# Pad rows written two tiles earlier and wider, and step counts read later, in a routed audio tower

## The chip, the cores and the metric

The kernel runs on one core of one Trainium2 chip. The metric is device time in microseconds, the median of several executions. TensorE (PE) multiplies, VectorE (DVE) and ScalarE (ACT) do elementwise work, GpSimd (POOL) does small scalar work and indirect transfers, SyncE (SP) issues ordinary transfers. Every engine follows its own list of instructions and meets the others at semaphores.

## The reference, cut to what matters

64 sequences of 125 tokens with 192 features pass through a token block (depthwise convolution, pointwise product, pooling to 62 tokens, a Fourier transform, a norm), attention with relative positions, a quantised feed-forward, a second local attention, and a mixture of experts. The change is at the border before the last part. There every token chooses one of 8 experts, whose gated feed-forward is applied to it alone:

```python
route = jax.nn.softmax(hidden_states @ router_w + router_b, axis=2)
max_prob = jnp.max(route, axis=2).reshape(-1, 1)
max_ind = jnp.argmax(route, axis=2).reshape(-1)
for e in range(N_EXPERTS):
    xe = jnp.where(mask, x, 0.0)
    oe = jax.nn.silu(xe @ w1[e]) * (xe @ w2[e]) @ w3[e]
out = out.astype(jnp.bfloat16) * max_prob
```

## The kernel before, in words

**First phase.** `TILES` is 32: a tile is two sequences, 124 real tokens in 128 lanes. `overlapped` runs the stages of all parts as a software pipeline, and each engine has its stages in an order written out by hand. Tiles are numbered 0 to 31. Three short stages at the end of the pipeline route a tile's tokens: `r_route` makes the logits, `r_choose` the one-hot choice, and `r_slots` on VectorE gives every token a row in the DRAM tensor `routed`, where each expert owns a region of `CAP` rows. `filled` holds the next free row of each region. `r_scatter` on GpSimd then writes the tile's rows to `routed` with an indirect transfer, from `moe_row`. That buffer is single, so `r_normalise_in` of the next tile waits on ScalarE for the scatter's landing (`r_scattered`). After the last router product TensorE runs `fill_bank(38)`, 38 products of the identity that nobody reads, and earlier fills of the same kind (`last_turns`) stand ahead of some stages of the last two tiles.

**Pad rows.** The experts work on whole blocks of 128 rows, so the rows behind each region's last token must hold pad rows. VectorE copies `filled` to `pads_at` in `r_slots` of tile 30, SyncE reads the eight places and writes two blocks (256 rows of 1,544 bytes) at each, and the scatter of tile 31 waits for all eight (`pads_written`), since it overwrites some of the pad rows with real ones.

**Plan and second phase.** After `r_slots` of tile 31 VectorE computes `plan`: for each expert step its expert and its first row, and the number of steps, here 34. `planned` releases all engines into `staggered`. Each engine reads three registers from `plan` (number of steps, last step, last but one: a `value_load` each), runs three peeled steps, then a loop over the rest, then the two closing steps. A step has three lagged parts: x (load 128 rows to `e_tok`, transpose, copy to `e_xT`, copy the expert's weights), g (two products to a hidden width of 512, and the gate: `e_gate_up`, `e_tanh_gate`, `e_silu`) and y (`e_down`, `e_finish`, `e_scatter`). In the peeled steps PE's list is: transpose of step 0; gate and up of step 0, transpose of step 1; gate and up of step 1, transpose of step 2, down of step 0. Then the loop opens with gate and up of step 2. SyncE waits for all 32 scatters before `staggered`, so before it reads any register.

Of the kernel before, what the change touches and what calls it, by code (L numbers as in the profile page):

```python
# [17 lines left out]
P = 128  # L18
TILES = NB // 2
# [17 lines left out]
NC = D // 2 + 1  # L37
CAP = 4224
MAX_TILES = TILES + NE
EARLY = 4  # L40
MAGIC = 1.5 * 2.0 ** 23
EPS = 1e-5
# [2 lines left out]
ROW = 2 * D + 2  # L45
# [4 lines left out]
def first(m):  # L50

    return isinstance(m, int) and m == 0
# [8 lines left out]
class Chain:  # L61
# [6 lines left out]
    def stage(self, name, m):  # L68
        if first(m):
            self.starts[name] = self.n  # L70
            return
        if self.per_tile is None:
            self.per_tile = self.n
        self.base, self.n = m * self.per_tile + self.starts[name], 0
# [14 lines left out]
def audio_tower(nc, x, taps, w_pw, b_pw, dft, dft_seq, gamma, beta,  # L89
# [3 lines left out]
    routed = nc.dram_tensor("routed", ((NE + 1) * CAP, ROW), FP32).ap()  # L93
# [3 lines left out]
    with ctx:  # L97
        def sb(name, shape, dt=FP32, mem=None):
            return (mem or ctx).enter_context(nc.sbuf_tensor(name, shape, dt))

        def sem(name):
            return ctx.enter_context(nc.semaphore(name))
# [5 lines left out]
        c_region = sb("c_region", [P, NE + 1])  # L108
        c_steps = sb("c_steps", [P, MAX_TILES])
        pad_rows = sb("pad_rows", [P, ROW])  # L110
        w3_sb = sb("w3_sb", [P, NE, HID1 // P, D])
        EXPERT, FIRST_ROW, STEPS = 0, MAX_TILES, 2 * MAX_TILES
        plan = sb("plan", [P, STEPS + 3], I32)
# [5 lines left out]
        earlier_tiles = sb("earlier_tiles", [P, NE + 1, NE])  # L119
        reached = sb("reached", [P, NE - 1, MAX_TILES])  # L120
        jumped = sb("jumped", [P, NE - 1, MAX_TILES])
        pads_at = sb("pads_at", [P, NE], I32)
# [6 lines left out]
        def lp(name, shape, dt=FP32):  # L129
            return sb(name, shape, dt, loop_mem)  # L130

        lp("early_weights", [P, EARLY, 3, HID1])

# [119 lines left out]
        def bank(name):  # L253
# [57 lines left out]
        planned, pads_written, pads_placed, w_early = (sem(k) for k in ("planned", "pads_written", "pads_placed", "early_weights_landed"))  # L311
        (e_loaded, e_xpose, e_xTr, e_lo_set, e_hi_set, e_g, e_u, e_tanhr, e_gated, e_yr, e_o, e_rested, e_final, e_turn, e_stored, all_stored) = (sem(f"e_{k}") for k in (
            "x_loaded", "transposed", "xT_ready", "low_weights_set", "high_weights_set", "gate_done", "up_done", "tanh_ready",
            "gated", "y_ready", "down_done", "rest_loaded", "row_final", "row_turn", "stored", "all_stored"))
        GE = NE - EARLY
        w_late = {e: sem(f"weights_landed_from_{e}") for e in range(EARLY, NE, GE)}
        w_ready = sem("expert_weights_ready")
        w_spare = sb("w_spare", [P, NE])

        def staggered(eng, stages):  # L320


            lag = {"x": 0, "g": 1, "y": 2}
            eng.wait_ge(planned, 1)
            total, last, last_but_one = (
                eng.value_load(plan[0:1, STEPS + k:STEPS + k + 1], min_val=TILES - 1 - k, max_val=MAX_TILES - k) for k in range(3))  # L326

            def body(steps):
                for name, stage in stages:
                    if name in steps:  # L330
                        stage(steps[name])
            for j in range(E_PEELED):
                body({name: j - late for name, late in lag.items() if j >= late})
            with eng.Fori(E_PEELED, total) as j:  # L334
                body({name: j - late for name, late in lag.items()})
            body({"g": last, "y": last_but_one})
            body({"y": last})
            return total
# [8 lines left out]
        def load_weights(queue, es, landed):  # L347

            for part, src, r in ((0, w1, slice(0, KB)), (1, w2, slice(KB, P))):
                queue.dma_start(w_sb[:, es, part, :], src[es, 0:P, :].rearrange("e p n -> p e n")).then_inc(landed, 16)  # L350
                queue.dma_start(w_sb[r, es, 2, :], src[es, P:D, :].rearrange("e p n -> p e n")).then_inc(landed, 16)
# [22 lines left out]
        def _(sp):  # L374
# [69 lines left out]
            sp.wait_ge(pads_placed, 1)  # L444
            for e in range(NE):
                at = sp.value_load(pads_at[0:1, e:e + 1], min_val=0, max_val=NE * CAP)  # L446
                sp.dma_start(routed[bass.ds(at, 2 * P), :].rearrange("(a p) w -> p a w", p=P),  # L447
                             pad_rows[:, :].unsqueeze(1).broadcast_to([P, 2, ROW])).then_inc(pads_written, 16)
            sp.wait_ge(r_scattered, 16 * TILES)

            def first_row(j):
                at = plan[0:1, FIRST_ROW + j:FIRST_ROW + j + 1] if isinstance(j, int) else plan[0:1, bass.ds(j + FIRST_ROW, 1)]
                return sp.value_load(at, min_val=0, max_val=NE * CAP)

            def load_rows(j):
                src = routed[bass.ds(first_row(j), P), 0:D]
                if not first(j):
                    sp.wait_ge(e_xpose, j)
                sp.dma_start(e_tok[:, :], src).then_inc(e_loaded, 16)

# [10 lines left out]
        def _(pool):  # L471
# [5 lines left out]
            for t_ in (kBD, p0, f_xqT, vBD, qT1, kBD_hi, p1, oT1, b_xT, r_xT):  # L477
                a = t_[tuple(slice(None) for _ in t_.shape)]
                last = pool.memset(a, 0.0)
# [31 lines left out]
            def spare_of(k):  # L511
                at = ("scatter", "rows").index(k)
                return pool_spare[:, at:at + 1]
# [41 lines left out]
            def r_scatter(m):  # L555
                pool.wait_ge(r_slot, m + 1)
                pool.wait_ge(r_row, m + 1)
                pool.wait_ge(b_kept, m + 1)
                if isinstance(m, int) and m == TILES - 1:
                    pool.wait_ge(pads_written, 16 * NE)  # L560

                pool.tensor_tensor(out=spare_of("scatter"), in0=half[:, :], in1=half[:, :], op=ALU.add)
                pool.indirect_dma_start(out=routed, out_offset=bass.IndirectOffsetOnAxis(ap=slot_now[:, 0:1], axis=0),  # L563
                                        in_=moe_row[:, :], in_offset=None).then_inc(r_scattered, 16)
# [4 lines left out]
            def mark_weights(landed, es):  # L569
                pool.wait_ge(landed, 64)  # L570
                for e in es:
                    pool.tensor_tensor(out=w_spare[:, e:e + 1], in0=half[:, :], in1=half[:, :], op=ALU.add).then_inc(w_ready, 1)  # L572
            mark_weights(w_early, range(EARLY))
            pool.wait_ge(r_scattered, 16 * TILES)
# [16 lines left out]
        def _(pe):  # L591
            def mm(dst, lhsT, rhs, start=True, stop=True):
                return nc.tensor.matmul(dst, lhsT, rhs, start=start, stop=stop)  # L593
# [29 lines left out]
            def fill_bank(times):  # L623

                pe.wait_ge(t_yread, TILES)
                for k in range(times):
                    mm(pt[:, 0:P], ident[:, :], ident[:, :])
# [262 lines left out]
            def r_rank(m):  # L890
# [9 lines left out]
                (2, a_add_relative), (1, t_dft_seq), (4, b_probs_transpose), (5, r_rank), (2, a_probs_transpose),  # L900
                (4, b_values), (2, a_values), (3, f_transpose_y), (4, b_transpose_o), (3, f_down),
                (2, a_transpose_heads), (4, b_output), (1, a_transpose)))
            fill_bank(38)

            def e_transpose(j):
                pe.wait_ge(e_loaded, 16 * j + 16)
# [33 lines left out]
        def _(act):  # L940
# [48 lines left out]
            def t_copy_z(m):  # L989
                if isinstance(m, int) and m == 2:  # L990
                    act.dma_start(w3_sb[:, :, :, :], w3.rearrange("e (k p) d -> p e k d", p=P)).then_inc(w_e, 16)
                    load_weights(act, slice(0, EARLY), w_early)
                act.wait_ge(t_z, 2 * m + 2)
# [196 lines left out]
        def _(dve):  # L1190
# [258 lines left out]
            def r_slots(m):  # L1449

                c = ch["r"]
                c.stage("slots", m)
                dve.wait_ge(r_ranked, m + 1)
                c.link(v.tensor_tensor(place[:, :], filled[:, :], pa0[:, RK:RK + NE + 1], ALU.add))
                c.link(v.tensor_tensor(filled[:, :], filled[:, :], pa0[:, TT:TT + NE + 1], ALU.add))
                v.scalar_tensor_tensor(place_one[:, :], place[:, :], 1.0, chosen[:, :], ALU.mult, ALU.mult,
                                       accum_out=slot_f[:, :]).then_inc(r_read, 1)
                dve.wait_ge(r_read, m + 1)
                dve.wait_ge(r_sum, m + 1)
                if isinstance(m, int) and m == TILES - 2:  # L1460
                    v.tensor_copy(pads_at[:, :], filled[:, 0:NE]).then_inc(pads_placed, 1)
                after_previous(dve, r_scattered, 16 * m)
                v.tensor_copy(slot_now[:, :], slot_f[:, :]).then_inc(r_slot, 1)
                at = c_tokens[:, m:m + 1] if isinstance(m, int) else c_tokens[:, bass.ds(m, 1)]
                v.tensor_copy(moe_row[:, TOKEN:ROW].bitcast(I32), at)
                v.reciprocal(moe_row[:, PROB:PROB + 1], exp_sum[:, :]).then_inc(r_row, 1)
# [23 lines left out]
            def by_step(t):  # L1490
                return t[:, 1:NE].unsqueeze(2).broadcast_to([P, NE - 1, MAX_TILES])
            plan_step(v.tensor_tensor(reached[:, :, :], c_steps[:, :].unsqueeze(1).broadcast_to([P, NE - 1, MAX_TILES]),
# [149 lines left out]
```

## Time and profile before

| | |
|---|---|
| median of 3 runs | 1183.44 us (1182.4 to 1183.57) |
| the profiled execution's own time | 1182.29 us |
| its span in the profile | 1180.4 us |
| PE busy | 1025.5 us (87%) |
| ACT busy | 835.4 us (71%) |
| DVE busy | 791.3 us (67%) |
| POOL busy | 363.6 us (31%) |
| mean granted TensorE clock | 0.98 |

Times in the rows are microseconds from the start of the span. A share of busy time is a mean over stages: the first phase takes about 985 us, the second some 190, and between them lies the stretch that the change touches, where the engines wait for one another.

### The profile page before, as it was taken

Reading aid. Unit: us, or ns where it says so; the run is one execution under the profiler, and the core shown is the slowest. Engines: PE = TensorE matmul, PEld = TensorE weight load, DVE = VectorE, ACT = ScalarE, POOL = GpSimd, SP = SyncE. Lnnn points to the kernel's source line nnn. Section 1 sums busy time; section 2 is a strip of 40 time slices with the busy share of each in tenths; the row PEclk is TensorE's granted clock in tenths of the full one; section 3 lists DMA queues with packets and bytes.
Section 4 is the critical chain, followed back from the end, with each engine's and each line's share of the span. In section 5 each row is a group of like instructions: output and inputs, shape, how many; then the busy total and the mean of one; then the engine's idle time right before and its main releaser. Section 6 shows DMA issues by size and latency. Waiting matters only on the chain. (4 is left out here: it accounts for less than half of the span.)

```text
span 1180.4 us, 31803 instructions
## 1 busy us (share of the span) xinstructions
PE 1025.5 (87%) x9700; PEld 787.8 (67%) x9733; DVE 791.3 (67%) x2641; ACT 835.4 (71%) x2673; POOL 363.6 (31%) x1096
## 2 busy tenths in 40 slices
PE   3748989999899999999888999989998887999995
PEld 2636666666666666666666666666666677888885
DVE  2346777777777777777777777777775542555553
ACT  2437888888888888888888888888887541333332
POOL 2012233333333333333333333333333211122222
PEclk9878999999999999999999999999999898999999
DMA  6153111111111111111111111111111403122221
GB/s 221 34 174 106 34 41 39 42 42 39 39 39 39 56 40 47 44 39 39 39 39 39 39 46 39 39 39 39 47 48 39 118 8 128 50 59 58 57 60 42
DMA packets 74258, 65.67 MB, mean 56 GB/s; under 512 B 39341, under 2 KB 63696, under 8 KB 74096
## 3 DMA queue, kind: packets, MB, share of 16 engines
q1 hardware_dynamic: 64832, 49.58, 14.3%
q0 software_dynamic: 3680, 9.38, 2.2%
q10 hardware_dynamic: 5712, 6.29, 1.8%
q8 instruction: 18, 0.29, 0.1%
q14 instruction: 16, 0.13, 0.0%
HBM read 36.57 MB, written 28.95 MB: 56 GB/s over the span
## 5 line engine op out<-in xcount | busy, mean ns | idle before, releaser
L1239 DVE SCALAR_TENSOR_TENSOR conv_lo<-xT_lo,c_taps,conv_lo 128x248 f32<-128x248 f32 x192 | 89.7, 467 | 14.9 <-ACT xT_hi L942 14.9
L1184 ACT ACTIVATE e_tanh<-bank_a 128x512 f32<-128x512 f32 x34 | 20.3, 597 | 104.7 <-PE bank_a L593 104.7
L1134 ACT ACTIVATE p<-bank_b,max 128x62 f32<-128x62 f32 x384 | 81.1, 351 | 0.2 <-DVE max L1404 0.2
L501 POOL TENSOR_TENSOR var_y<-ssq_y,c_eps 128x1 f32<-128x1 f32 x32 | 6.0, 189 | 233.6 <-ACT f_sq L1104 233.6
L593 PE MATMUL bank_a<-e_xT,w_now 128*128 128x128 f32 x544 | 70.5, 284 | 5.8 <-DVE e_gate L1516 1.5
L593 PEld LDWEIGHTS bank_a<-e_xT,w_now 128*128 128x128 f32 x544 | 64.9, 196 | 14.9 <-issue 12.0
L593 PE MATMUL bank_a<-c_wv,a_xT 64*64 64x384 f32 (+1 forms) x512 | 74.0, 503 | 0.0
L593 PE MATMUL bank_a<-a_xT,c_wq 64*128 64x128 f32 (+1 forms) x512 | 71.7, 282 | 0.0
L593 PE MATMUL bank_a<-c_wo,oT 128*128 128x192 f32 x384 | 68.5, 329 | 0.3 <-ACT oT L942 0.2
L593 PE MATMUL bank_a<-a_xT,c_wk 64*128 64x128 f32 (+1 forms) x512 | 68.8, 280 | 0.0
L593 PEld LDWEIGHTS bank_a<-a_xT,c_wq 64*128 64x128 f32 (+1 forms) x512 | 64.3, 191 | 4.3 <-ACT a_xT L942 0.4
L1404 DVE TENSOR_REDUCE max<-bank_b 128x8 f32<-128x496 f32 x64 | 31.9, 540 | 50.2 <-PE bank_b L593 50.2
L1243 DVE SCALAR_TENSOR_TENSOR conv_hi<-xT_hi,c_taps,conv_hi 128x124 f32<-128x124 f32 x192 | 65.4, 340 | 0.0
L593 PEld LDWEIGHTS bank_a<-c_wo,oT 128*128 128x128 f32 x384 | 62.1, 191 | 1.3 <-ACT oT L942 0.8
L1511 DVE COPY w_now<-w_sb 128x512 f32 x34 | 14.5, 427 | 71.9 <-PE bank_a L593 68.8
L593 PEld LDWEIGHTS bank_a<-a_xT,c_wk 64*128 64x128 f32 (+1 forms) x512 | 62.1, 190 | 0.0
L1040 ACT ACTIVATE p<-bank_a,max 128x62 f32<-128x62 f32 x256 | 55.5, 331 | 7.7 <-DVE max L1301 7.7
L593 PEld LDWEIGHTS bank_t<-z_sb,c_dft_seq 128*128 128x128 f32 x256 | 32.7, 199 | 34.4 <-ACT z_sb L942 33.9
L593 PE MATMUL bank_b<-c_wqkv,b_xT 128*128 128x288 f32 x128 | 39.6, 432 | 16.1 <-ACT b_xT L942 16.0
L593 PE MATMUL bank_b<-w_sb,e_y 128*128 x272 | 50.0, 327 | 2.1 <-DVE e_row L1531 2.0
L593 PEld LDWEIGHTS bank_a<-c_wv,a_xT 64*64 64x64 f32 (+1 forms) x512 | 22.3, 133 | 36.5 <-issue 36.5
L593 PE MATMUL bank_t<-z_sb,c_dft_seq 128*128 128x95 f32 (+1 forms) x256 | 37.9, 293 | 9.3 <-ACT z_sb L942 8.3
(264 smaller groups left out, 3059.5 us busy)
## 6 DMA issues: line engine op xcount, KB each, us to landing
rel_scores<-rel_tok SPq DMA_DIRECT2D x32, 492.0 KB, 2.6
rel_skew<-rel_scores SPq DMA_DIRECT2D x64, 124.0 KB, 3.0
x_tok<-in_x SPq DMA_DIRECT2D x32, 187.5 KB
e_rest<-routed SPq DMA_DIRECT2D x34, 97.0 KB, 1.9
e_tok<-routed SPq DMA_DIRECT2D x34, 96.0 KB, 2.0
routed<-pad_rows SPq DMA_DIRECT2D x8, 386.0 KB, 3.8
w_sb<-in_w ACTq DMA_DIRECT2D x1, 3072.0 KB, 12.3
w_sb<-in_w ACTq DMA_DIRECT2D x2, 1024.0 KB, 13.7
```

The lines of the kernel that those rows point to most:

```text
L501: pool.tensor_tensor(out=var[k][:, :], in0=ssq[k][:, :], in1=c_eps[:, width:width + 1], op=ALU.mult).then_inc(var_eps[k], 1)
L593: return nc.tensor.matmul(dst, lhsT, rhs, start=start, stop=stop)
L1040: last = nc.scalar.activation(p0[:, h, 0:T], pa1[:, h * T:(h + 1) * T], ACT.Exp, bias=max0[:, h:h + 1])
L1134: last = nc.scalar.activation(p1[:, h, 0:T], src[:, at * T:(at + 1) * T], ACT.Exp, bias=max1[:, mx:mx + 1])
L1184: nc.scalar.activation(e_tanh[:, :], pa0[:, :], ACT.Tanh, scale=0.5).then_inc(e_tanhr, 1)
L1239: c.mark(v.scalar_tensor_tensor(conv_lo[:, :, :], xT_lo[:, :, k:k + PAIRS], c_taps[:, 0, k:k + 1], conv_lo[:, :, :], ALU.mult, ALU.add))
L1243: ins = v.scalar_tensor_tensor(conv_hi[:, :], xT_hi[:, k:k + PAIRS], c_taps[:, 1, k:k + 1], conv_hi[:, :], ALU.mult, ALU.add)
L1404: last = v.tensor_reduce(max1[:, lo:lo + n], src[:, 0:n * T].rearrange("p (h s) -> p h s", h=n), axis=AX.X, op=ALU.max, negate=True)
L1511: v.tensor_copy(w1_now[:, :], weights_of(e, 0)).then_inc(e_lo_set, 1)
```

## The change

Three edits. First, the pad rows' places are taken in `r_slots` of tile 29 and not of tile 30; since two more tiles can now fill rows behind them, three blocks are written at each place and not two; and the scatter of tile 30 waits for them, not that of tile 31. Second, `staggered` reads its three registers behind the three peeled steps on every engine, and SyncE's wait for the 32 scatters moves into `load_rows` of step 0, behind the reading of its first row. Third, the last fill is 33 products and not 38.

```diff
+PADDED_AT, PAD_BLOCKS = TILES - 3, 3
...
             eng.wait_ge(planned, 1)
-            total, last, last_but_one = (
-                eng.value_load(plan[0:1, STEPS + k:STEPS + k + 1], min_val=TILES - 1 - k, max_val=MAX_TILES - k) for k in range(3))
...
             for j in range(E_PEELED):
                 body({name: j - late for name, late in lag.items() if j >= late})
+            total, last, last_but_one = (
+                eng.value_load(plan[0:1, STEPS + k:STEPS + k + 1], min_val=TILES - 1 - k, max_val=MAX_TILES - k) for k in range(3))
             with eng.Fori(E_PEELED, total) as j:
...
-                sp.dma_start(routed[bass.ds(at, 2 * P), :].rearrange("(a p) w -> p a w", p=P),
-                             pad_rows[:, :].unsqueeze(1).broadcast_to([P, 2, ROW])).then_inc(pads_written, 16)
-            sp.wait_ge(r_scattered, 16 * TILES)
-
+                sp.dma_start(routed[bass.ds(at, PAD_BLOCKS * P), :].rearrange("(a p) w -> p a w", p=P),
+                             pad_rows[:, :].unsqueeze(1).broadcast_to([P, PAD_BLOCKS, ROW])).then_inc(pads_written, 16)
...
-                if not first(j):
+                if first(j):
+                    sp.wait_ge(r_scattered, 16 * TILES)
+                else:
                     sp.wait_ge(e_xpose, j)
...
-                if isinstance(m, int) and m == TILES - 1:
+                if isinstance(m, int) and m == PADDED_AT + 1:
                     pool.wait_ge(pads_written, 16 * NE)
...
-            fill_bank(38)
+            fill_bank(33)
...
-                if isinstance(m, int) and m == TILES - 2:
+                if isinstance(m, int) and m == PADDED_AT:
                     v.tensor_copy(pads_at[:, :], filled[:, 0:NE]).then_inc(pads_placed, 1)
```

## Rows read from the trace of the kernel before

**Rows 1.** Timeline of ACT, `r_normalise_in` of tiles 30 and 31.
```profile
961.79 0.55 ACT L1066 ACTIVATE moe_row<-res_m,norm_shift_b,rstd_b 128x192 f32<-128x192 f32 x1
...
980.25 0.55 ACT L1066 ACTIVATE moe_row<-res_m,norm_shift_b,rstd_b 128x192 f32<-128x192 f32 x1 [5.74 <-DMA routed<-moe_row,slot_now]
```
**Rows 2.** Timeline of POOL; in brackets the idle time before and its releaser.
```profile
975.24 1.04 POOL L563 DMA_INDIRECT routed<-moe_row,slot_now  x1 [0.49 <-issue]
...
977.62 0.19 POOL L525 TENSOR_TENSOR norm_shift_b<-neg_mean_b,rstd_b 128x1 f32<-128x1 f32 x1
989.18 0.19 POOL L562 TENSOR_TENSOR pool_spare<-half 128x1 f32<-128x1 f32 x1 [11.37 <-DMA routed<-pad_rows]
...
992.66 1.01 POOL L572 TENSOR_TENSOR w_spare<-half 128x1 f32<-128x1 f32 x4 [1.10 <-DMA routed<-moe_row,slot_now]
```
**Rows 3.** Timeline of SP, merged: first start and time to the last.
```profile
975.72 9.79 SPq L447 DMA_DIRECT2D routed<-pad_rows  x8
994.97 9.96 SPq L459 DMA_DIRECT2D e_tok<-routed  x3
```
**Rows 4.** Chain of waits, 980 to 1016: start, us, what ran.
```profile
985.13 3.89 DMA routed<-pad_rows
```
**Rows 5.** Timeline of DVE: start, us, engine, line, operation, out<-in.
```profile
952.74 0.15 DVE L1463 CAST slot_now<-slot_f 128x1 int32<-128x1 f32 x1 [0.97 <-DVE place_one L1456]
...
974.06 0.17 DVE L1461 CAST pads_at<-filled 128x8 int32<-128x8 f32 x1
...
984.85 0.15 DVE L1466 RECIPROCAL moe_row<-exp_sum 128x1 f32<-128x1 f32 x1
...
989.30 0.20 DVE L1503 CAST plan<-plan_f 128x83 int32<-128x83 f32 x1
```
**Rows 6.** Timeline of PE around the border of the two phases.
```profile
975.32 3.96 PE L593 MATMUL bank_t<-ident 128*128 128x128 f32 x34
980.85 0.44 PE L596 MATMUL bank_a<-ident,moe_row 128*128 128x128 f32 x2 [1.58 <-ACT moe_row L1066]
...
983.93 8.73 PE L593 MATMUL bank_t<-ident 128*128 128x128 f32 x76
996.96 0.44 PE L596 MATMUL bank_t<-ident,e_tok 128*128 128x128 f32 x2 [4.30 <-DMA e_tok<-routed]
...
1005.93 2.02 PE L593 MATMUL bank_a<-e_xT,w_now 128*128 128x128 f32 x16 [1.51 <-DVE e_gate L1516]
```
**Rows 7.** Stretches: us, then busy us of PE, PEld, DVE, ACT, POOL; PEclk, DMA share, GB/s.
```profile
976.00:988.00 12.00, 10.12 (x88) 9.55 (x87) 5.10 (x26) 1.63 (x6) 1.35 (x5) 1.00 0.79 282
915.40:922.20 6.80, 4.14 (x35) 2.80 (x34) 4.69 (x12) 6.40 (x27) 0.93 (x3) 1.00 1.02 274
905.10:911.90 6.80, 4.70 (x38) 2.69 (x34) 3.87 (x12) 6.20 (x20) 2.55 (x11) 1.00 0.18 74
922.20:929.00 6.80, 6.53 (x75) 5.75 (x76) 2.69 (x14) 3.58 (x9) 0.98 (x2) 0.50 0.69 191
...
998.20:1004.02 5.82, 5.82 (x33) 5.37 (x34) 0.00 (x0) 0.60 (x1) 0.00 (x0) 0.50 0.06 17
1010.82:1013.97 3.15, 3.15 (x33) 2.91 (x34) 1.44 (x4) 0.10 (x2) 1.01 (x2) 1.00 0.18 46
```
**Rows 8.** Instructions reading `plan`: ns min/median/max, first and last start (us).
```profile
L453 SPq TENSOR_LOAD <-plan x68: 262/268/281, 994.3 to 1164.9; - x68
```
**Rows 9.** Line L326, the three register reads of each engine, same columns.
```profile
L326 DVEq SEQ_ASSERT  x3: 23/23/41, 990.4 to 991.6; - x3
L326 PEldq TENSOR_LOAD <-plan x3: 305/492/545, 990.6 to 992.4; - x3
...
L326 PEldq SEQ_ASSERT  x3: 18/18/28, 991.4 to 993.0; - x3
```
**Rows 10.** Line L334, setting up and running the loop, 1005 to 1016.
```profile
L334 PEldq MOVE  x3: 34/38/43, 1009.2 to 1014.8; - x3
```
**Rows 11.** Line L342, the reading of a step's expert, 985 to 1016.
```profile
L342 DVEq SEQ_ASSERT  x4: 23/23/23, 992.3 to 1012.6; - x4
```

## The prediction

> **What bounds the kernel now.** I read the chain of waits first, then the timelines of each engine from 950 to 1016, then the instructions that read `plan`, then busy time by stretch. The first phase (to about 985) and the expert loop (from gate and up of step 2, then a steady 1010.82 − 1005.93 = 4.9 us per step [rows 6, 7]) have TensorE almost always busy, and no edit touches what a step does. What the edits can win lies in the border between them. There the reader sees four waits in a row.
>
> First, `r_normalise_in` of tile 31 starts at 980.25, after 5.74 us of idle ScalarE, and what releases it is the landing of tile 30's scatter [rows 1]. That scatter was issued at 975.24, half a microsecond before the first pad write [rows 2, 3], and shared the transfer engines with them. Its own operand was ready at 977.62 + 0.19 = 977.81 [rows 2].
> Second, the last pad write is issued at 985.13 and lands 3.89 later [rows 4]; only then, at 989.18 after 11.37 idle, does GpSimd begin tile 31's scatter [rows 2], though its row was complete at 984.85 + 0.15 = 985.00 [rows 5]. It lands before 992.66 [rows 2], so 3.48 after its start, with little else in flight.
> Third, SyncE wakes there, reads three registers and a first row, and issues the first `e_tok` at 994.97 [rows 3]. The plan had stood since 989.30 + 0.20 = 989.50 [rows 5].
> Fourth, TensorE has run out of fills, waits 4.30 us, starts the first transpose at 996.96 [rows 6], and does gate and up of step 0 at a granted clock of 0.50 in 5.82 us, where step 2 has 1.00 and 3.15 us [rows 7].
>
> **Edit 1, pads by tile 29's places.** The copy to `pads_at` moves from 974.06 to about 952.74 [rows 5]. The first pad write followed it by 975.72 − 974.06 = 1.66 [rows 3], so it now goes out at 954.4. Eight writes of 3 × 128 × 1,544 bytes are 4.74 MB against 3.16 MB. In 976 to 988 the engines moved 282 GB/s at a busy share of 0.79 [rows 7]; at that rate 4.74 MB take 16.8 us, and with about 1.5 us ahead of the first packets the last lands near 972.7. Tile 30's scatter starts its first instruction at 974.5. So the new wait costs nothing, by 1.8 us. Bounds: at the mean of the old series, 3.16 MB in 989.02 − 975.72 = 13.3 us, it is 20 us and lands at 974.4, still in time; at a full share of 282/0.79 = 357 GB/s it lands near 969. Queued behind that wait on GpSimd is `b_scale` of tile 31, for which `r_normalise_in` waits, but TensorE is in fills until 975.32 + 3.96 = 979.28 [rows 6], which covers the first half microsecond or so of lateness.
> The writes now collide with tile 29's scatter. Tile 30's, so disturbed, landed 980.25 − 975.24 = 5.0 after issue. Tile 29's goes out near 953.9; at 5.0 it lands at 958.9, and even at 5.0 × 1.5 at 961.4, while `r_normalise_in` of tile 30 starts at 961.79 for other reasons [rows 1]. Cost nothing, cover 0.4 to 2.9 us.
> Tile 30's scatter now lands 3.48 after its first instruction at 974.55, at 978.03, so `moe_row` starts 2.2 earlier. Not all of it arrives: the transposes that started 0.60 after it, at 980.85 [rows 6], would start at 978.63 but stand behind the fills to 979.28. Gain 980.85 − 979.28 = **1.57**, carried through logits, ranks, `r_slots` and the plan, which is ready at 987.93. The scatter of tile 31 starts 0.14 behind its row, at 983.57, and lands at 987.05, before the plan.
>
> **Edit 2, registers behind the peeled steps.** SyncE now goes from the plan to the first row. Reading it and issuing takes 994.97 − 994.3 = 0.67 [rows 3, 8]. A first read after the same wake-up can be slow: 545 ns on TensorE against 305 [rows 9], so up to 0.24 more. I take 0.77: `e_tok` goes out at 988.70, and its scatter wait is met since 987.05. That is 6.27 earlier than 994.97, so beyond the 1.57 it is **4.70**. VectorE's first weights, which had the three reads ahead of them too, come earlier by as much as is needed, and ScalarE's are far ahead.
> The reads themselves come back later. TensorE's took from 990.6 to 993.0, 2.4 us, in three of 305 to 545 ns and their arithmetic [rows 9]. Its sequencer has given out all of step 0's down product by 1009.2 [rows 10], 1.6 us before the array starts gate and up of step 2 at 1010.82 [rows 7]. If the reads take 1.9 us (three at 305 ns) to 2.4, that start slips by 0.4 to 1.0, with 0.1 to 0.2 to dispatch. VectorE's reads end at 991.6 [rows 9], 2.1 after the plan; behind its step-2 work they push the expert's reading, done at 1012.6 before [rows 11], to 1014.4 to 1014.7, 0.2 to 0.5 past its need at about 1014.2 (TensorE ends step 2's products at 1013.97 [rows 7]), and lie beside TensorE's delay. SyncE's, ScalarE's and GpSimd's lie in idle time. I take **−0.6**; bounds are 0, all hidden, and −2.4, TensorE's reads in full.
> The Trainium skill, "TensorE: Matmul & The Clock Gate", section "Architectural detail: the array is 16× 32×32, not 1× 128×128", gives TensorE a queue of 64 entries, so its sequencer could run far ahead and the reads would cost nothing; the sum would then be 0.6 larger, 1174.5. The trace agrees that it runs ahead, but by the 1.6 us above.
>
> **Edit 3, fills.** 38 took 8.73, so 0.230 each [rows 6]; 33 take 7.58 and end at 983.93 − 1.57 + 7.58 = 989.94. The first transpose, with `e_tok` landing as before 1.99 after issue, starts at 990.69. TensorE idles 0.75 and not 4.30, then 0.8 for ScalarE's copy as before. The granted clock was 1.00 until the long idle, so I expect gate and up of step 0 at 1.00: 5.82 − 3.15 = **2.67**. Bounds: 0 and 2.67.
>
> **Sum.** 1.57 + 4.70 + 2.67 − 0.6 = 8.34. The profiled execution took 1182.29, 1.89 more than its span of 1180.4; it would take 1173.95. It is 1.15 below the median of the runs, 1183.44, so the median becomes 1183.44 − 8.34 = **1175.1**, 0.7% less. This kernel's measurement tells about 0.2%, 2.4 us, from no change.
>
> **Rivals.**
> *The clock falls later* (0.28). The low clock of 922.2 to 929 followed no long idle, only a stretch with 4.14 us of matmuls in 6.8; after 4.70 in 6.8 it stayed at 1.00 [rows 7]. From the end of the fills to gate and up of step 1 (1005.93 before [rows 6], now 996.99) there would be 0.44 + 3.15 + 0.5 = 4.1 in 7.05. That resembles the stretch before a fall. Step 1 would then run low in place of step 0, giving 2.67 back and a little of the down product: 2.9, so 1178.0. For it speaks that stretch; against it that the fills before are dense. It may differ between executions. The Trainium skill, same page, section "HAM oscillation — how this bites in real kernels", blames long waits of TensorE between its bursts; none of the new gaps (0.75, 0.8, 1.5) is as long as 4.30, so by that rule the clock stays and 1175.1 holds.
> *Reads in series* (0.06). TensorE's 2.4 and VectorE's 2.1 add instead of overlapping: −4.5 in place of −0.6, 1179.0. Against it: VectorE had its expert's number 1.6 us ahead of its need [rows 11], and that slack takes most of its reads.
> *Pads late* (0.07). If the bigger writes run at 200 GB/s they land near 978.1 with their start, 2.9 past what costs nothing: 1178.0.
> *Slower than before* (0.02). The same wait, worse: all of 8.34 is gone when pads land near 983.5, 29 us after their first issue, an average of 163 GB/s. Rows show 238 over the old series, so it decides only below two thirds of that.
> *The gain does not come* (0.04). Something else releases the first `e_tok`, for instance SyncE held by full queues, and only what the scatter gains remains: around 1181.
>
> **Chances and range.** Forecast 0.53; its own range is 1174.0 to 1176.8, from reads at 0 to −1.0, a first read between 0.67 and 0.91 and half a microsecond of spread between medians. With the clock rival, the series and the late pads, 1173.6 to 1179.3 leaves out about 1 in 10. Faster by over 0.2% (below 1181.1) 0.94, within 0.04, slower 0.02.
>
> **What would show it.** Right: pads issued from about 954.4 and landed before 974.5; `moe_row` of tile 31 at about 978.0, the transposes at 979.3; plan at 987.9; first `e_tok` at 988.7, first transpose at 990.7 with under 1 us idle; gate and up of step 0 in 3.2 us at 1.00; a gap of 0.4 to 1.0 on TensorE ahead of gate and up of step 2, and 4.9 per step after. Wrong: GpSimd idle on pads ahead of tile 30's scatter, `moe_row` of tile 30 released by a transfer, a granted clock of 0.50 after 990, or a step period other than 4.9.

## The result and the profile after

Six executions of the changed kernel have a median of 1175.02 us (1174.04 to 1176.97), six of the kernel before 1183.11 (1182.4 to 1183.57). The ratio is 0.9934, 95% interval 0.9921 to 0.9947. The profiled execution took 1174.49 us with a span of 1172.7. The forecast was 1175.1.

In this execution the whole border sits later by 962.28 − 961.79 = 0.49. `moe_row` of tile 29 was already 0.47 later (938.20 against 937.73), and the first instruction that an edit moves, the copy to `pads_at`, ran at 953.24, so this offset is not the edits' doing. So below I measure from `moe_row` of tile 30, the first of these two rows (the timeline of ScalarE, beside [rows 1]):

```profile
962.28 0.55 ACT L1067 ACTIVATE moe_row<-res_m,norm_shift_b,rstd_b 128x192 f32<-128x192 f32 x1
...
978.76 0.55 ACT L1067 ACTIVATE moe_row<-res_m,norm_shift_b,rstd_b 128x192 f32<-128x192 f32 x1 [3.75 <-DMA routed<-moe_row,slot_now]
```

Tile 30's is released by no transfer, so the collision of the larger writes with tile 29's scatter cost nothing. Tile 31's is still released by the scatter of tile 30, but 16.48 us behind tile 30's row and not 18.46. That scatter now lands 978.76 − 975.99 = 2.77 after it was issued, where it took 5.01 with the pad writes behind it [rows 1, 2]. The timeline of GpSimd (beside [rows 2]):

```profile
974.99 0.20 POOL L563 TENSOR_TENSOR pool_spare<-half 128x1 f32<-128x1 f32 x1 [15.28 <-DVE moe_row L1467]
975.99 1.04 POOL L564 DMA_INDIRECT routed<-moe_row,slot_now  x1 [0.81 <-issue]
...
978.13 0.19 POOL L526 TENSOR_TENSOR norm_shift_b<-neg_mean_b,rstd_b 128x1 f32<-128x1 f32 x1
983.85 0.20 POOL L563 TENSOR_TENSOR pool_spare<-half 128x1 f32<-128x1 f32 x1 [5.53 <-DVE moe_row L1467]
...
987.31 0.63 POOL L573 TENSOR_TENSOR w_spare<-half 128x1 f32<-128x1 f32 x4 [0.82 <-DMA routed<-moe_row,slot_now]
```

Both scatters now start when VectorE has made their row (the brackets name `moe_row`), neither waits for pads, and the second lands before 987.31, ahead of the plan. VectorE and SyncE (beside [rows 5] and [rows 3]):

```profile
988.08 0.20 DVE L1504 CAST plan<-plan_f 128x83 int32<-128x83 f32 x1
```
```profile
954.90 11.86 SPq L448 DMA_DIRECT2D routed<-pad_rows  x8
989.02 7.32 SPq L460 DMA_DIRECT2D e_tok<-routed  x3
```

The first `e_tok` follows the plan by 989.02 − 988.28 = 0.74, where 5.47 lay between them [rows 3, 5]. The pad writes land 4.2 to 5.6 after issue, so the last, issued at 966.4, by 972.0, 3 us before the scatter of tile 30 could want them:

```profile
L448 SPq DMA_DIRECT2D routed<-pad_rows x8: 372/372/415, 954.9 to 966.4; - x8
...
DMA to landing us min/median/max: 4.2/5.3/5.6
```

TensorE (beside [rows 6]):

```profile
975.82 3.96 PE L594 MATMUL bank_t<-ident 128*128 128x128 f32 x34
979.61 0.38 PE L597 MATMUL bank_a<-ident,moe_row 128*128 128x128 f32 x2
...
982.64 7.61 PE L594 MATMUL bank_t<-ident 128*128 128x128 f32 x66
991.05 0.41 PE L597 MATMUL bank_t<-ident,e_tok 128*128 128x128 f32 x2 [0.80 <-DMA e_tok<-routed]
992.32 2.05 PE L594 MATMUL bank_a<-e_xT,w_now 128*128 128x128 f32 x16 [0.86 <-ACT e_xT L943]
...
997.25 2.02 PE L594 MATMUL bank_a<-e_xT,w_now 128*128 128x128 f32 x16 [1.41 <-DVE e_gate L1517]
...
1003.14 2.02 PE L594 MATMUL bank_a<-e_xT,w_now 128*128 128x128 f32 x16 [1.11 <-DVE e_gate L1517]
```

The router's transposes stand directly behind the fills. The wait for `e_tok` is 0.80 and not 4.30. Gate and up of step 0 run at full clock (stretches, beside [rows 7]):

```profile
992.32:995.50 3.18, 3.18 (x33) 2.94 (x34) 0.00 (x0) 0.64 (x2) 0.00 (x0) 1.00 0.12 31
```

What is new is the gap of 1.11 ahead of gate and up of step 2. It is TensorE's register reads (beside [rows 9] and [rows 10]):

```profile
L334 PEldq TENSOR_LOAD <-plan x3: 302/311/317, 1000.8 to 1002.1; - x3
...
L334 PEldq SEQ_ASSERT  x3: 18/18/18, 1001.4 to 1002.7; - x3
...
L334 DVEq TENSOR_LOAD <-plan x3: 298/304/310, 1003.4 to 1004.6; - x3
```
```profile
1001.68 0.68 DVE L1517 SCALAR_TENSOR_TENSOR e_gate<-e_tanh,bank_a 128x512 f32<-128x512 f32 x1
...
1003.11 1.86 PEld L594 LDWEIGHTS bank_a<-e_xT,w_now 128*128 128x128 f32 x16 [1.38 <-issue]
```

The gap's bracket in the timeline of TensorE names `e_gate` of step 1, but that was ready at 1002.36. In the kernel before the next product follows `e_gate` by 0.14, here by 0.78, and the weight load ahead of it waited for nothing but its own issue. VectorE's reads begin at 1003.4, when gate and up already run.

From gate and up of step 3 to the end of the span it is 1172.7 − 1008.05 = 164.65 us, against 1180.4 − 1015.72 = 164.68. The loop is the same.

### The profile page after: what moved, and what is told of

It is laid out like the page before. It is cut to its first block and busy times, and to the rows that moved or that the text cites. A ratio compares the mean times of both kernels' runs of the same rounds, so it can differ in the third digit from the quotient of the medians.

```text
span 1172.7 us, 31784 instructions
## 1 busy us (share of the span) xinstructions
PE 1022.0 (87%) x9690; PEld 784.3 (67%) x9723; DVE 791.9 (68%) x2641; ACT 836.8 (71%) x2673; POOL 364.9 (31%) x1096
```

## The experiments

All from the changed kernel unless said. The times come from three chips: one for the first four kernels below (pads only, reads only, SyncE behind, 38 fills), one for 14 fills, the gap fills, 15 fills and five blocks, one for the tiny fills, 24 fills, the changed kernel again and the last one. On them the kernel before has medians of 1186.1 to 1187.6 and spreads over 4.8 to 6.9 us, not 1183.1 and 1.2 as in the first result, so I give ratios to the kernel before on the same chip, and beside them a length from each profile: the **border**, from `moe_row` of tile 30 to the start of gate and up of step 3. It is 1015.72 − 961.79 = 53.93 in the kernel before and 1008.05 − 962.28 = 45.77 in the changed one. One profile is one execution, so what the clock did in it is told too. A **fall** is a stretch in which the granted clock drops from 1.00 to 0.50.

### Edit 1 alone, edit 2 alone

Pads only is the kernel before, with

```diff
+PADDED_AT, PAD_BLOCKS = TILES - 3, 3
...
-                if isinstance(m, int) and m == TILES - 1:
+                if isinstance(m, int) and m == PADDED_AT + 1:
...
-                if isinstance(m, int) and m == TILES - 2:
+                if isinstance(m, int) and m == PADDED_AT:
```

and `PAD_BLOCKS` blocks in place of two in each pad write. Reads only is the kernel before, with the two lines of `total, last, last_but_one` moved behind the peeled steps, and

```diff
-            sp.wait_ge(r_scattered, 16 * TILES)
...
-                if not first(j):
+                if first(j):
+                    sp.wait_ge(r_scattered, 16 * TILES)
+                else:
```

Both keep the 38 fills of the kernel before.

> Edit 1 alone: places taken in tile 29, three blocks, scatter of tile 30 waits; the registers are read ahead of the peeled steps and there are 38 fills, as before. My theory: the pads' wait held both the scatter of tile 31 and, by collision, moe_row of tile 31, so the plan comes 1.3 to 1.6 us earlier and SyncE, now released by the plan, reads three registers (1.65) and a first row (0.7): first e_tok some 4.5 us earlier than in the kernel before, fills end after the landing of the plan and leave about 1 us idle, the clock stays at 1.00 (2.67): together about 7 us, ratio 0.994. Rival, that the late reading on SyncE was the main bound: then this alone gives 2 us or less, ratio 0.998.

> Edit 2 alone: registers behind the peeled steps and SyncE's wait for the scatters behind the first row's reading; pads as before, 38 fills. My theory: the scatter of tile 31 still lands at about 992.6, the first e_tok goes out 0.3 behind it, 2.0 us earlier than before; TensorE pays 1.0 us ahead of gate and up of step 2; the idle behind the fills shrinks from 4.3 to 2.3 us, so the clock may or may not fall: gain 1 us with the fall, 3.7 without, ratio 0.999 or 0.997. Rival: with the reads out of the way the gain is as large as that of both edits, ratio 0.993.

Measured: pads only 0.9938 (0.9917 to 0.9959), reads only 0.9980 (0.9967 to 0.9993). The timelines of SyncE, first of pads only and then of reads only:

```profile
992.24 8.90 SPq L460 DMA_DIRECT2D e_tok<-routed  x3
```
```profile
993.66 7.31 SPq L459 DMA_DIRECT2D e_tok<-routed  x3
```

From `moe_row` of tile 30 (963.82 and 962.87) the first `e_tok` goes out after 28.42 and 30.79, against 33.18 before and 26.74 with both: 4.8 earlier by the pads alone, 2.4 by the reads alone, 6.4 by both. The pads were the main bound, as the first expectation says. The collision is told apart too: tile 30's scatter landed 2.78 after issue with the pads moved (977.51 to 980.29) and 4.76 with the pads as before (976.33 to 981.09). The borders are 49.77 and 49.90. The profile of pads only had the clock fall twice, in steps 0 and 1, which cost 1.8 and 1.6 (6.71 and 6.49 between starts of gate and up, where the undisturbed ones are 4.93 and 4.90). That of reads only had it fall once, at 982 to 988, among the fills. There it cost little, since the slow fills took time in which TensorE would have waited: the wait for `e_tok` was 0.97, not the 2.3 expected, and gate and up of step 0 ran at 1.00. So the two borders don't compare the edits, the `e_tok` times do. The ratios set reads only apart from both edits, but not pads only (0.9938 against 0.9934): what edit 2 adds to edit 1 is seen in the traces and not in the times. In reads only the gap ahead of step 2 was there too: 5.99 between gate and up of steps 1 and 2.

### Which reads may stand behind

Four engines read the counts ahead of the peeled steps again, and SyncE alone behind them:

```diff
-        def staggered(eng, stages):
+        def staggered(eng, stages, ahead=True):
+            def step_counts():
+                return [eng.value_load(...) for k in range(3)]
+            if ahead:
+                total, last, last_but_one = step_counts()
...
-            total, last, last_but_one = (
+            if not ahead:
+                total, last, last_but_one = step_counts()
...
-            staggered(sp, (("x", load_rows), ("y", load_rest)))
+            staggered(sp, (("x", load_rows), ("y", load_rest)), ahead=False)
```

> The changed kernel, but only SyncE reads its registers behind the peeled steps; the other four read them ahead, TensorE in the time of its fills. My theory: the 1.0 us gap ahead of gate and up of step 2 goes, and nothing takes its place, since VectorE (reads 2.1, expert 0.9, weights 0.85 after the plan) has the first weights just as e_xT is ready: 1 us under the changed kernel, about 1174.0, ratio to the kernel before 0.9925. Rival: VectorE's first weights come late by up to 1 us and the time stays at that of the changed kernel.

Measured: 0.9926 (0.9910 to 0.9943). Its profile has 4.90 between gate and up of steps 1 and 2, so the gap is gone. VectorE (its timeline) has the first weights ready at 991.95 + 0.42 = 992.37, and gate and up start at 992.59:

```profile
991.60 0.43 DVE L1516 COPY w_now<-w_sb 128x512 f32 x1 [3.02 <-issue]
991.95 0.42 DVE L1517 COPY w_now<-w_sb 128x512 f32 x1
```

So the rival's late VectorE didn't come, by 0.2 us. But in this execution the clock fell in gate and up of step 0 (6.66 between starts, 1.7 lost), and the border is 46.46. The gain of 1.0 is clear in the trace; the ratios of 0.9926 and 0.9934 don't tell it from nothing. The edit took the reads away from four engines at once; that TensorE's were the ones that counted is read from the timeline of the changed kernel above.

### The fills and the clock

The changed kernel with another number of fills ahead of step 0, here 38, below 14 and 24:

```diff
-            fill_bank(33)
+            fill_bank(38)
```

> The changed kernel with 38 fills in place of 33. The five fills take 1.15 us and end 0.35 us behind the landing of e_tok: 0.3 us slower than the changed kernel if fills only fill, with no idle behind them. If the busy time of TensorE in the border decides the clock in some executions (the changed kernel's runs spread over 2.9 us), the spread narrows and the median is the same or up to 0.5 us lower.

Measured: 0.9930 (0.9909 to 0.9950), border 45.98, 0.2 longer than with 33; no fall in the border. So edit 3 is worth nearly nothing by itself. In four executions the spread was 2.1.

> The changed kernel with 14 fills behind the router and not 33, so that TensorE idles about 5 us ahead of the first transpose. Nothing else waits for the fills. My theory (2.67 of the gain was the clock): the granted clock is 0.50 during gate and up of step 0, which takes 5.8 us in place of 3.2, and the kernel is 2.7 us slower than the changed one: ratio to the kernel before 0.9957. From the moe_row of tile 30 to gate and up of step 3 the changed kernel takes 45.8 us; this takes 48.4. Rival, the shorter idle bought nothing by itself: no difference, ratio 0.993.

Measured: 1.0063 (1.0041 to 1.0085), 15 us slower than the changed kernel, where 2.7 was expected. The border accounts for little of it: 47.76, 2.0 longer, from 5.10 of idle and a low clock in the first half of step 0. The rest is in the loop: 30 steps from gate and up of step 3 take 163.91 and not 146.87 (149.2 to 150.9 in the other kernels on this chip). Nearly every one takes about 5.47 and not 4.90. Lines of its timeline for one such step:

```profile
1024.91 0.17 PEld L597 LDWEIGHTS bank_t<-ident,e_tok 128*128 128x128 f32 x2
...
1025.02 0.60 ACT L1185 ACTIVATE e_tanh<-bank_a 128x512 f32<-128x512 f32 x1 [2.71 <-PE bank_a L594]
...
1025.72 0.43 DVE L1512 COPY w_now<-w_sb 128x512 f32 x1 [2.36 <-PE bank_a L594]
...
1026.40 0.68 DVE L1517 SCALAR_TENSOR_TENSOR e_gate<-e_tanh,bank_a 128x512 f32<-128x512 f32 x1
...
1027.23 2.18 PE L594 MATMUL bank_a<-e_xT,w_now 128*128 128x128 f32 x16 [0.57 <-DVE e_gate L1517]
```

And of the same place in a step of the changed kernel:

```profile
1020.98 0.60 ACT L1185 ACTIVATE e_tanh<-bank_a 128x512 f32<-128x512 f32 x1 [3.02 <-PE bank_a L594]
...
1021.23 0.43 DVE L1512 COPY w_now<-w_sb 128x512 f32 x1 [1.77 <-PE bank_a L594]
...
1021.91 0.68 DVE L1517 SCALAR_TENSOR_TENSOR e_gate<-e_tanh,bank_a 128x512 f32<-128x512 f32 x1
```

ScalarE answers TensorE's gate and up at once in both. VectorE starts the next weights 0.25 behind ScalarE's tanh in the changed kernel and 0.70 with 14 fills. `e_gate` stands behind the weights on VectorE, and TensorE waits for it. The change that was made touches TensorE's code ahead of the loop only.

> The changed kernel with 4 full fills and 29 products of one column by one column behind the router: as many instructions on TensorE as with 33 fills, but only some 3 us of work, so that it idles 4 us or more ahead of the first transpose. With 14 fills the steps of the loop took 5.45 us in place of 4.90, because VectorE woke 0.45 later after TensorE's gate and up. Theory A, the number of instructions on TensorE ahead of the loop decides that (where its code lies): here steps take 4.90 again and only the clock's price is left, about 2.7 us, ratio 0.9957. Theory B, the idle time or the fall of the clock ahead of the loop sets the rhythm of the steps: 5.45 again, ratio about 1.006.

```diff
-            fill_bank(33)
+            fill_bank(4)
+            for k in range(29):
+                mm(pt[0:1, 0:1], ident[:, 0:1], ident[:, 0:1])
```

Measured: 0.9947 (0.9928 to 0.9966), border 47.95. Five of its 30 steps take about 5.44 and the others 4.90. TensorE idled longer than with 14 fills, and the low clock lasted longer:

```profile
981.67 2.66 PE L594 MATMUL bank_t<-ident 128*128 128x128 f32 x66
990.17 0.66 PE L597 MATMUL bank_t<-ident,e_tok 128*128 128x128 f32 x2 [5.85 <-DMA e_tok<-routed]
991.70 3.79 PE L594 MATMUL bank_a<-e_xT,w_now 128*128 128x128 f32 x16 [0.86 <-ACT e_xT L945]
995.41 1.18 PE L594 MATMUL bank_a<-e_xT,w_hi_now 64*128 64x128 f32 x16
```

So theory B falls, as far as one profile and four executions on another chip can tell: neither the idle time nor the clock sets the rhythm of the steps. What is left is the number of TensorE's instructions ahead of the loop, or something that follows from it. The price of the idle time is here 2.2 of border (47.95 against 45.77), below the 2.7 expected, since the clock came back before the second half of step 0's products. It is a price only against an execution without a fall; the second profile of the changed kernel, below, has 47.57.

> The changed kernel with 24 fills. TensorE idles about 2.9 us ahead of the first transpose. Theory A (number of instructions): steps between 4.90 and 5.45, depending on where the code comes to lie; theory B (idle time): a fall of the clock in about half of the executions and with it 5.45. Without either: ratio 0.9945, the clock's price in half of the executions.

Measured: 0.9959 (0.9946 to 0.9973), border 47.56, with the clock low in gate and up of step 0 (6.52 between starts) after 2.86 idle. Eight of 30 steps are slow, where the other kernels on these chips have four to seven. So if the number of instructions acts, it does not act evenly: with 14 fills nearly every step is slow, with 24, 33 and 38 few are.

The changed kernel was then run once more on one of these chips, with no edit.

> The changed kernel itself, on the chip of the other three: ratio to the kernel before 0.9934 as at first. Its own profile tells how often a step takes 5.45 here, and whether the clock falls in the border.

Measured: 0.9932 (0.9916 to 0.9949), as at first. But its profile is not the first one. The border is 47.57, 1.8 longer, in the same code, after an idle of 0.94 where the first had 0.80. The stretch of gate and up of step 0:

```profile
990.56:995.29 4.73, 4.73 (x33) 4.38 (x34) 0.00 (x0) 0.63 (x1) 0.00 (x0) 0.64 0.08 21
```

4.73 us at a mean granted clock of 0.64, against 3.18 at 1.00. This is the clock rival in an execution of the changed kernel itself, though in step 0 and not in step 1. Seven of its 30 steps are slow (150.67 us in place of 146.87), where the profiles of the first result have none, before or after. The six executions spread over 4.1 us, the 13 of the kernel before on this chip over 4.8.

### Filling the gaps, and two fills fewer

Both kernels have SyncE's reads alone behind the peeled steps, as above, and more fills, among them 3 and 5 behind the transposes of steps 0 and 1:

```diff
-            fill_bank(33)
+            fill_bank(36)
+            def fill_gap(times):
+                for k in range(times):
+                    mm(pf0[:, 0:P], ident[:, :], ident[:, :])
...
+                if isinstance(j, int) and j < 2:
+                    fill_gap((3, 5)[j])
```

The second has 15 fills ahead of the router's transposes as well:

```diff
-                          "r_transpose": (0, 17)
+                          "r_transpose": (0, 15)
```

> The kernel with only SyncE's registers behind the peeled steps, 36 fills, and 3 and 5 more fills (into a bank that is free) behind the transposes of steps 0 and 1, so that TensorE has almost no idle time from the router to the loop. If short falls of the clock there cost the time that the executions spread by (the profile of the kernel without these fills had 0.50 in 3.4 us of steps 0), the clock stays at 1.00 in every execution and the median falls by 0.8 to 1.6 us: ratio to the kernel before 0.9915. If the fills only stand in the way: no gain, 0.9926.

> As the kernel with the gap fills, and 15 instead of 17 fills ahead of the router's transposes of tile 31, which stood behind their end at 979.8 while moe_row was ready from about 979.3. Two fills are 0.46 us: the plan 0.4 us earlier, the time 0.4 us less, if the fills are what bounds there; nothing if moe_row is. Ratio to the kernel before 0.9911.

Measured: gap fills 0.9927 (0.9907 to 0.9947), border 44.93; with 15 fills besides 0.9917 (0.9900 to 0.9934), border 45.35, of which 0.47 is one slow step. Between gate and up of steps 1 and 2 both have 4.90, so the 1.0 of the reads is in their borders. In neither profile did the clock fall in the border. The executions still spread, over 5.3 us in the first and 2.3 in the second, so the clock in the border is not the whole of their spread; slow steps of 0.55 each are another part. A gain from the gap fills was not measured. The two fills ahead of the transposes gave little here: the transposes of tile 31 start 17.28 after `moe_row` of tile 30 with 15, 17.33 with 17. The shorter fills end before `moe_row` of tile 31 is ready, and TensorE waits 0.23 for it:

```profile
979.26 0.44 PE L601 MATMUL bank_a<-ident,moe_row 128*128 128x128 f32 x2 [0.23 <-ACT moe_row L1077]
```

In this execution `moe_row` of tile 31 itself started 16.68 behind tile 30's, 0.2 later than in the others. The last kernel, where it was 16.44, has the transposes at 17.04, so there the two fills gave 0.3. It leaves the gap fills out again and keeps the rest:

```diff
-            fill_bank(33)
+            fill_bank(35)
...
-                          "r_transpose": (0, 17)
+                          "r_transpose": (0, 15)
...
-            staggered(sp, (("x", load_rows), ("y", load_rest)))
+            staggered(sp, (("x", load_rows), ("y", load_rest)), ahead=False)
```

> Only SyncE's registers behind the peeled steps, 15 fills ahead of the router's transposes of tile 31 and 35 at the end: as many as in the changed kernel, no gap fills. Against the changed kernel on the same chip 1.0 us from the reads and 0.4 from the two fills: ratio to the kernel before 0.992, against 0.9934. If the reads' 1.0 is only taken over by a late VectorE, the two are the same.

Measured: 0.9929 (0.9910 to 0.9948), border 44.73, the shortest of all, 1.04 under the changed kernel's first profile, with no fall. The 1.04 is 0.99 from the reads and 0.19 from an earlier step 0, less 0.15: gate and up of steps 0 and 1 lie 5.08 apart and not 4.93, as in the two kernels above. On that chip the changed kernel had 0.9932. The 1.0 us is seen in the trace and lost in the spread of the executions.

### Pads that are late

```diff
-PADDED_AT, PAD_BLOCKS = TILES - 3, 3
+PADDED_AT, PAD_BLOCKS = TILES - 3, 5
```

> The changed kernel with five blocks of pad rows at each place and not three: 7.9 MB and not 4.7, which lands about 11 us later, near 983. My theory of the late pads: the scatter of tile 30 then waits on GpSimd with b_scale of tile 31 behind it, and of about 8.4 us of lateness against 974.5 all but some 0.7 goes into the time: ratio to the kernel before 1.000 (0.998 to 1.002). Rival: the engines move the writes faster than with three blocks (357 GB/s), then they land near 978 and cost 3 us, ratio 0.996.

Measured: 0.9991 (0.9977 to 1.0005), border 54.35. The timeline of GpSimd:

```profile
980.37 0.20 POOL L563 TENSOR_TENSOR pool_spare<-half 128x1 f32<-128x1 f32 x1 [21.01 <-DMA routed<-pad_rows]
```

The pads landed at about 980.2, 25.7 us after the first issue (954.53): 7.9 MB at some 307 GB/s, between the two expectations. The scatter of tile 30 started 5.7 us later than in the changed kernel (18.44 after `moe_row` of tile 30, against 12.71), and the border grew by 8.6. The transposes were 5.45 later; the rest came with low clocks, 1.5 from the transposes to gate and up of step 0, behind an idle of 5.30, and 1.6 in step 0. So the rival "pads late" has its price, in this execution more than one for one, but three blocks stayed 3 us clear of it.

## Why the prediction was right

Each length from `moe_row` of tile 30, before and after, from the rows.

- **Pads and collision, forecast 1.57.** The plan's copy starts at 989.30 − 961.79 = 27.51 and 988.08 − 962.28 = 25.80: 1.71. The path was the one forecast: `moe_row` of tile 31 gained 1.98, and the fills ahead of the transposes took the rest. That the pads held it by collision is borne out by pads only and reads only.
- **First row behind the plan, forecast 4.70.** `e_tok` at 33.18 and 26.74, 6.44, less the 1.71: 4.73. SyncE took 0.74 from the plan to the issue; 0.77 was taken.
- **The clock, forecast 2.67.** Between the starts of gate and up of steps 0 and 1, 7.73 and 4.93: 2.80, of which 5.82 − 3.18 = 2.64 is gate and up themselves. The other 0.16 is `e_gate`, ready 1.60 behind the products and not 1.76; the kernels with VectorE's reads ahead again have the 1.76. But this holds for the execution without a fall. In the second profile of the same kernel it was 6.51, so 1.22.
- **The reads, forecast −0.6.** Between steps 1 and 2, 4.89 and 5.89: −1.00. This is the term that was mis-sized. The reads took the least that was foreseen (1000.8 to 1002.7, 1.9 us), but they started 3.55 behind gate and up of step 1, not 3.27 as the loop entry did before, and from the last of them to the first matmul passed another 0.44, in which TensorE set up its loop, where 0.1 to 0.2 was taken. VectorE was late there too, its copies of the weights 0.61 and not 0.25 behind ScalarE's tanh, but ahead of its own reads, and inside TensorE's delay.
- **Sum, forecast 8.34.** 8.16 in the border, with −0.07 between the first `e_tok` and gate and up of step 0 and −0.01 behind step 2. The medians differ by 8.09. That the sum came so near is in part luck: the reads' 0.40 too little was made up by 0.30 in the other three terms, and the profile measured had no fall, where the prediction gave the forecast 0.53 and the fall 0.28.

The clock rival was put as one of two outcomes and is both: one profile of the changed kernel has the fall and one doesn't. The spread of 2.9 us against 1.2 in the first result would fit that, but no trace of those other executions shows it, and slow steps may add to it. Its price was 1.6, not 2.9, in the execution seen, and it struck step 0 and not step 1: the low clock took about 4.73 × (1.00 − 0.64) / 0.50 = 3.4 us of gate and up of step 0, where the kernel before had it through all of their 5.82 [rows 7]. The prediction weighed long waits of TensorE between its bursts as the cause of a fall, from the Trainium skill, "TensorE: Matmul & The Clock Gate", section "HAM oscillation — how this bites in real kernels". They don't explain that profile: its longest wait in the border is 1.42 us, behind the fall, and 0.94 ahead of it. The queue of 64 entries that the Trainium skill, same page, section "Architectural detail: the array is 16× 32×32, not 1× 128×128", gives TensorE did not hide the reads either. With the reads of four engines ahead of the steps the 1.0 us was gone.

Pads late and slower than before did not come. Five blocks show both: with pads at 980.2 nearly the whole gain was gone (0.9991, border 54.35 against 53.93 before), where the prediction put that point at 983.5, since it left out the low clocks that such a wait brings. Reads in series did not come: the whole gap ahead of step 2 is 1.0 where 4.5 was the price, and from step 2 on each start follows the last by 4.9.

## What to carry to other kernels

A wait is worth following to the transfers it collides with: the pads held the path at two places, one of them a scatter that never named them, and a move of one tile emptied both. Ask of every instruction that is moved under what it lay: ahead of the steps TensorE's register reads lay under its fills, behind them they cost 1.0 us once, and SyncE alone needed them moved. And measure a span between two fixed events in the profile beside the whole time, since gains of 1 us drown in what the executions do elsewhere, and look whether the clock fell in it before you compare two profiles.

## What the runs showed of the hardware that was not expected

- **Slow steps.** A step of the loop takes 4.90 or about 5.45 us. In the slow one VectorE starts later behind TensorE's last product, while ScalarE starts on time. The two profiles of the first result, before and after, have none; the others have 4 to 8 in 30 for every kernel but one; with 14 fills it is 29 of 30. The two may not be the same thing: the scattered slow steps have VectorE 0.77 to 0.84 behind ScalarE's tanh, those with 14 fills 0.65 to 0.71, the others 0.25. Four full fills and 29 tiny ones, as many instructions as with 33 fills, had 5. That it hangs on the number of TensorE's instructions ahead of the loop rests on this pair only, and the two ran on different chips. Where the code or the data come to lie, or how VectorE waits, was not tried, and the cause stays open.
- **One late start.** In step 1 VectorE starts its copies 0.61 or 0.62 behind ScalarE's tanh in every profile with the reads behind the peeled steps on all engines, and 0.24 or 0.25 in every other, at a time when no read of its own has begun. The cause is open too.
- **Short falls.** The granted clock fell in gate and up of step 0 in the second profile of the changed kernel, with no wait of TensorE above 0.94 us in the 10 us ahead of it, and not in the first, which ran the same code with a wait of 0.80. With 24 fills it fell there after a wait of 2.86, and in reads only it fell among the fills, at 982 to 988, behind a wait of 1.33. The kernel with SyncE's reads alone behind had a fall in step 0 too, and the three built on it had none. One profile each doesn't show that those edits prevent it.
